# Another order for the first tiles of a four-layer adaptive FFN kernel: router weights loaded first, scores behind tile 0's router, mixing and first diagonal product inside convolutions, weights' transposes at tile 2

## The reference

```
x = x + L0_ffn(L0_cond(x, c))
x = x + L1_ffn(L1_cond(x, c))
x = x + L2_ffn(L2_cond(x, c))
x = x + L3_ffn(L3_cond(x, c))
```

## Time and profile before

| | us |
|---|---|
| median of 3 runs | 742.98 |
| lowest, highest | 742.76, 746.0 |
| the profiled execution, its own time | 743.95 |
| its span, first to last instruction | 742.2 |
| TensorE busy | 727.5 (98% of the span) |
| VectorE, ScalarE, GpSimd busy | 462.0, 300.0, 344.8 |

### The profile page before, as it was taken

How to read it: one execution, slowest core, us unless ns; L and a number is a source line. 1 busy time by engine, 2 the same in 40 slices (tenths; PEclk the granted TensorE clock), 3 DMA queues, 4 the chain that set the end, 5 groups by cost and what they waited for, 6 DMA issues and landing times.

```text
span 742.2 us, 11037 instructions
## 1 busy us (share of the span) xinstructions
PE 727.5 (98%) x3550; PEld 591.3 (80%) x3566; DVE 462.0 (62%) x1060; ACT 300.0 (40%) x577; POOL 344.8 (46%) x386
## 2 busy tenths in 40 slices
PE   9899999999999999999999999999999999999997
PEld 5687777877788888888888888877788887888886
DVE  4976667678622345663477345886678888755533
ACT  5644445444432333254334334232544344534321
POOL 3556677676425512121221015867654645464630
PEclk9999999999999999999999999999999999999999
DMA  8666447544051022110220102424513212221200
GB/s 277 130 139 172 151 135 213 157 143 143 29 184 57 29 62 80 58 29 1 86 99 16 30 37 64 170 58 128 172 44 114 73 44 72 59 87 44 72 29 29
DMA packets 44775, 68.91 MB, mean 93 GB/s; under 512 B 21248, under 2 KB 21600, under 8 KB 44464
## 3 DMA queue, kind: packets, MB, share of 16 engines
q1 hardware_dynamic: 34816, 37.77, 16.9%
q0 software_dynamic: 9152, 29.69, 13.1%
q10 hardware_dynamic: 752, 0.74, 0.3%
HBM read 45.03 MB, written 17.65 MB: 84 GB/s over the span
## 4 chain that ended last, share of the span: by engine, by line
PE 82%; DVE 5%; POOL 5%; DMA 3%; issue 3%; ACT 1%; SPq 0%; DVEq 0%; POOLq 0%; ACTq 0%
PE bank L2232 21%; PE bank L2215 13%; PE bank L2183 12%; PE bank L2088 11%; PE bank L1873 8%; PE bank L1804 4%; PE bank L1909 3%; PE bank L2194 2%; POOL wur L698 2%; PE bank L1943 2%; DMA tap<-in_x_taps_dram 1%; DMA raw<-in_w_dram 1%; PE bank L1921 1%; PE bank L2045 1%; PE bank L2108 1%
## 5 line engine op out<-in xcount | busy, mean ns | idle before, releaser
L1656 DVE TENSOR_TENSOR sil<-bank,sil 128x512 f32<-128x512 f32 x56 | 38.6, 689 | 95.2 <-PE bank L2232 95.2
L2232 PE MATMUL bank<-th,wgr 128*128 128x512 f32 x224 | 88.3, 394 | 1.0 <-DVE tl L1444 1.0
L2232 PE MATMUL bank<-th,wur 128*128 128x512 f32 x224 | 87.7, 391 | 0.0
L2088 PE MATMUL bank<-wda,hh 128*128 128x512 f32 x224 | 87.6, 391 | 0.0
L2232 PE MATMUL bank<-tl,wgr 128*128 128x512 f32 x224 | 87.4, 390 | 0.0
L2232 PE MATMUL bank<-tl,wur 128*128 128x512 f32 x224 | 87.3, 390 | 0.0
L2088 PE MATMUL bank<-wda,hl 128*128 128x512 f32 x224 | 87.3, 390 | 0.0
L2183 PE MATMUL bank<-wda,xch 128*128 (+1 forms) x272 | 84.6, 393 | 0.0
L1111 ACT ACTIVATE hh<-sil 128x512 fp32r<-128x512 f32 x56 | 35.4, 632 | 115.2 <-DVE sil L1656 115.2
L1103 ACT ACTIVATE sil<-bank 128x512 f32<-128x512 f32 x56 | 33.4, 597 | 93.8 <-PE bank L2232 93.7
L1658 DVE TENSOR_TENSOR hl<-sil,hh 128x512 fp32r<-128x512 f32 x56 | 46.3, 826 | 39.1 <-ACT hh L1111 39.1
(11 more groups left out here) (365 smaller groups left out, 1782.4 us busy)
## 6 DMA issues: line engine op xcount, KB each, us to landing
tap<-in_x_taps_dram SPq DMA_DIRECT2D x16, 260.0 KB, 2.9
xin<-in_x_rows_dram SPq DMA_DIRECT2D x16, 256.0 KB, 3.1
xd<-xo SPq DMA_DIRECT2D x16, 256.0 KB, 3.2
xc<-xd SPq DMA_DIRECT2D x16, 256.0 KB, 4.2
xres<-xd SPq DMA_DIRECT2D x4, 1024.0 KB, 5.5
xd<-xres SPq DMA_DIRECT2D x4, 1024.0 KB, 5.0
tsd<-tf SPq DMA_DIRECT2D x4, 1024.0 KB, 4.2
raw<-in_w_dram POOLq DMA_DIRECT2D x16, 256.0 KB, 3.1
```

What stands on the lines that cost most here:

```text
L1656: v.tensor_tensor(hf[:, m % 2], p_pre[(2 * m + 1) % 3][:], sil[:, m % 2], ALU.mult).then_inc(s_hf, 1)
L2088: last = mm(p_acc[j][:], h[:, m % HSLOTS, j * P:(j + 1) * P], wda[:, m * D:(m + 1) * D], start=(m == 0 and n == 0), stop=(m == MT - 1 and ...
L2232: last = mm(p_pre[(2 * m + b) % 3][:], w[:, (m * KT + kt) * P:(m * KT + kt + 1) * P], x[:, kt], start=(kt == 0 and n == 0), stop=(kt == KT ...
```

## The change

The loads are issued in another order and partly from another queue: the router weights and the MLP tensors right behind tap 0 on SyncE, the three condition tensors on ScalarE's queue; the rest of the mixing matrices go ahead of w1_raw. Fewer filler matmuls are issued (12, 2 and 2, where there were 14, 4, 4 and 3). conv(t) does its nine matmuls grouped by part (hi x hi, hi x lo, lo x hi) instead of by shift, for all tiles, and can call another function after the first group: mixed(0) inside conv(2), mix1(0) inside conv(3). lora(t) is grouped by part too and waits for its low part only before the last group. scores go behind router(0), mixing_weights behind router(1), mixed(1) and mixed(2) behind conv(2) and lora(1). hidden(0) goes ahead of positions(1). weights_t and scales_t stand between conv(3) and base(2), the copies to wq are made by ScalarE instead of VectorE, and the scales use bank 4 instead of bank 6. The lists of the other engines follow: w0_hi on ScalarE goes ahead of hid2 and of gate_exp(0), an activation that loads the exponent table stands behind w0_hi(1), weight_scales on VectorE goes to tile 1's step ahead of hidden_lo(1), softmax_two behind t0_lo(1), and GpSimd does x1_lo(0), x1_bias(0) and tap_lo(3) before the weight rounds, and the first table product between the third and fourth round.

```diff
--- before.py
+++ after.py
...
             load_tap(0)
-            sp.dma_start(condt[:], cond_t).then_inc(d_cond, 16)
-            sp.dma_start(cw4[:], cw_t).then_inc(d_cond, 16)
-            sp.dma_start(fs4[:], fside).then_inc(d_cond, 16)
             sp.dma_start(ga_raw[:], l0_ga).then_inc(d_ga, 16)
+            sp.dma_start(mw01[:], mlp_w01).then_inc(d_mlp, 16)
+            sp.dma_start(mw2[:], mlp_w2).then_inc(d_mlp, 16)
+            sp.dma_start(mb01[:], mlp_b01).then_inc(d_mlp, 16)
+            sp.dma_start(mb2[:], mlp_b2.partition_broadcast(BATCH)).then_inc(d_mlp, 16)
+            load_tap(1)
+            sp.dma_start(w0_raw[:], l0_w).then_inc(d_w0, 16)
             sp.dma_start(mixr[:, 0], mix_w[:, 0]).then_inc(d_mix, 16)
-            sp.dma_start(w0_raw[:], l0_w).then_inc(d_w0, 16)
-            load_tap(1)
             sp.dma_start(lb_raw[:], l0_lb).then_inc(d_lb, 16)
+            load_tap(2)
             load_xin(0)
+            sp.wait_ge(d_mix, 16)
+            sp.dma_start(mixr[:, 1:], mix_w[:, 1:]).then_inc(d_mix, 16)
             sp.dma_start(w1_raw[:], l1_w).then_inc(d_w1, 16)
             load_xin(1)
             sp.dma_start(b1b[:], l1_b.partition_broadcast(P)).then_inc(d_b1b, 16)
-            load_tap(2)
-            sp.wait_ge(d_mix, 16)
-            sp.dma_start(mixr[:, 1:], mix_w[:, 1:]).then_inc(d_mix, 16)
...
             rounded(w0h[:, 3], w0_raw[:, 3], s_w0p)
-            pool.wait_ge(s_mix, 2)
+            pool.wait_ge(d_mix, 16)
+            rounded(mixh[:, 0], mixr[:, 0], s_mixh)
             pool.wait_ge(s_hm, 1)
             pool.wait_ge(d_mix, 32)
-            rounded(mixh[:, 1:], mixr[:, 1:], s_mix)
+            rounded(mixh[:, 1:], mixr[:, 1:], s_mixh)
             tap_lo(2)
+            x1_lo(0)
+            x1_bias(0)
+            tap_lo(3)
             pool.wait_ge(s_sw, 1)
-            for k in range(KT):
+
+            def weight_round(k):
                 nc.gpsimd.tensor_scalar(w1_raw[:, k], w1_raw[:, k], wsc[:, 2, k:k + 1], MAGIC, ALU.mult, ALU.add).then_inc(s_wqf, 1)
-            x1_lo(0)
+
+            weight_round(0)
+            weight_round(1)
+            weight_round(2)
             diag_tile(0)
+            weight_round(3)
             diag_lo(0)
-            tap_lo(3)
             diag_tile(1)
-            x1_bias(0)
...
             act.dma_start(conv_raw[:], conv_w).then_inc(d_conv, 16)
-            act.dma_start(mw01[:], mlp_w01).then_inc(d_mlp, 16)
-            act.dma_start(mw2[:], mlp_w2).then_inc(d_mlp, 16)
-            act.dma_start(mb01[:], mlp_b01).then_inc(d_mlp, 16)
-            act.dma_start(mb2[:], mlp_b2.partition_broadcast(BATCH)).then_inc(d_mlp, 16)
+            act.dma_start(condt[:], cond_t).then_inc(d_cond, 16)
+            act.dma_start(cw4[:], cw_t).then_inc(d_cond, 16)
+            act.dma_start(fs4[:], fside).then_inc(d_cond, 16)
...
             t0_hi(0)
+            tap_hi(1)
+            act.wait_ge(d_w0, 16)
+            w0_hi(0)
             act.wait_ge(s_m1, 2 * COND_LAYERS + 1)
             for l in range(COND_LAYERS):
                 nc.scalar.activation(hid2[:, l], bank[6][:, l * BATCH:(l + 1) * BATCH], ACT.Gelu,
                                      bias=mb01[:, l, 1:2]).then_inc(s_g1, 1)
-            tap_hi(1)
-
-            def w0_hi(k):
-                nc.scalar.activation(w0h[:, k], w0_raw[:, k], ACT.Copy).then_inc(s_w0s, 1)
+            w0_hi(1)
+            nc.scalar.activation(rt[:, 192:193], ones[:, 0:1], ACT.Exp)
...
                 x1_hi(t - 1)
                 diag_hi1(t - 1)
+                if t == 2:
+                    for k in range(KT):
+                        act.wait_ge(s_wqt, k // 2 * 2 + 2)
+                        nc.scalar.activation(wq[:, k], bank[6 - k // 2][:].bitcast(BF16)[:, (k % 2) * D:(k % 2 + 1) * D],
+                                             ACT.Copy).then_inc(s_wqc, 1)
                 gate_exp(t)
...
+            gate_exp(0)
             act.wait_ge(s_at, 1)
             nc.scalar.activation(atte[:], att[:], ACT.Exp).then_inc(s_g1, 1)
-            act.wait_ge(d_w0, 16)
-            w0_hi(0)
-            gate_exp(0)
-            w0_hi(1)
+            act.wait_ge(d_lb, 16)
+            nc.scalar.activation(lbh[:], lb_raw[:], ACT.Copy).then_inc(s_lbs, 1)
             conv_out(1)
             act.wait_ge(s_const, 9)
             nc.scalar.activation(identb[:], ident[:], ACT.Copy).then_inc(s_atc, 1)
+            hidden_hi(0)
+            t0_hi(1)
+            tap_hi(2)
             act.wait_ge(s_att, 1)
             nc.scalar.activation(attt[:].rearrange("k l b -> k (l b)"), bank[5][0:3 * CH, 0:COND_LAYERS * BATCH],
                                  ACT.Copy).then_inc(s_atc, 1)
-            act.wait_ge(d_lb, 16)
-            nc.scalar.activation(lbh[:], lb_raw[:], ACT.Copy).then_inc(s_lbs, 1)
-            t0_hi(1)
-            hidden_hi(0)
             mixed(0)
-            tap_hi(2)
+            x1_hi(0)
+            gate_exp(1)
+            conv_out(2)
+            tap_hi(3)
             mixed(1)
-            gate_exp(1)
-            x1_hi(0)
-            conv_out(2)
-            mixed(2)
-            tap_hi(3)
-            diag_hi1(0)
             t0_hi(2)
             hidden_hi(1)
+            mixed(2)
+            diag_hi1(0)
             mixed1(0)
             for t in range(2, TILES):
...
...
                 gating(t, t - 2 if t >= 2 else None)
                 gated(t)
                 if t == 1:
-                    weight_integers()
+                    weight_scales()
                 hidden_lo(t)
                 if t + 1 < TILES:
                     t0_lo(t + 1)
                 if t == 1:
                     for k in range(KT):
-                        dve.wait_ge(s_wqt, k // 2 * 2 + 2)
-                        v.tensor_copy(wq[:, k], bank[6 - k // 2][:].bitcast(BF16)[:, (k % 2) * D:(k % 2 + 1) * D]).then_inc(s_wqc, 1)
+                        dve.wait_ge(s_wqf, k + 1)
+                        v.tensor_scalar(wq_rows[:, k], w1_raw[:, k], MAGIC, QMAX, ALU.subtract, ALU.min).then_inc(s_wqr, 1)
                 if t >= 2:
...
+            w0_lo(0)
+            w0_lo(1)
+            gating(0, None)
+            w0_lo(2)
             softmax_one()
-            softmax_two()
-            gating(0, None)
-            for k in range(KT):
-                w0_lo(k)
+            w0_lo(3)
             gated(0)
             dve.wait_ge(s_lbs, 1)
             v.tensor_tensor(lbl[:], lb_raw[:], lbh[:].bitcast(F32), ALU.subtract).then_inc(s_lbs, 1)
             hidden_lo(0)
             t0_lo(1)
-            mix_rows(slice(1, COND_LAYERS), 3)
-            weight_scales()
+            softmax_two()
+            mix_rows(slice(0, 1), 1)
+            mix_rows(slice(1, COND_LAYERS), 2)
             for t in range(1, TILES):
                 step(t)
...
+            def conv(t, between=None):
+
+                pe.wait_ge(s_taph, t + 1)
+                pe.wait_ge(s_cvw, 1)
                 if t >= 1:
                     pe.wait_ge(s_cvs, t)
-                n = 0
-                for s in range(SHIFTS):
-                    for w, x in parts((cvh[:, s], cvl[:, s]), (taph[:, :, s:s + P], tapl[:, :, s:s + P])):
-                        last = mm(p_cv[:].rearrange("p (b n) -> p b n", b=BPT), w, x, start=(n == 0), stop=(n == 3 * SHIFTS - 1))
-                        n += 1
+                for n, (w, x) in enumerate(((cvh, taph), (cvh, tapl), (cvl, taph))):
+                    if n == 1 and between:
+                        between()
+                    if n == 1:
+                        pe.wait_ge(s_tapl, t + 1)
+                    if n == 2 and t == 0:
+                        pe.wait_ge(s_cvw, 2)
+                    for s in range(SHIFTS):
+                        last = mm(p_cv[:].rearrange("p (b n) -> p b n", b=BPT), w[:, s], x[:, :, s:s + P],
+                                  start=(n == 0 and s == 0), stop=(n == 2 and s == SHIFTS - 1))
                 last.then_inc(s_cv, 1)
...
+            def side_scale():
...
+            keep_busy(12)
             conv(0)
-            pe.wait_ge(d_cond, 48)
-            mm(bank[7][:, 0:BATCH], cw4[:], condt[:], start=True, stop=True).then_inc(s_m1, 1)
+            side_scale()
             pe.wait_ge(d_mlp, 64)
             for l in range(COND_LAYERS):
                 mm(bank[5][:, l * BATCH:(l + 1) * BATCH], mw01[:, l, 0], condt[:], start=True, stop=True).then_inc(s_m1, 1)
-            keep_busy(4)
+            keep_busy(2)
             pe.wait_ge(s_const, 9)
             positions(0)
             pe.wait_ge(s_g1, COND_LAYERS + 1)
             for l in range(COND_LAYERS):
                 mm(bank[6][:, l * BATCH:(l + 1) * BATCH], mw01[:, l, 1], hid1[:, l], start=True, stop=True).then_inc(s_m1, 1)
-            keep_busy(4)
+            keep_busy(2)
...
+                pe.wait_ge(s_hth, t + 1)
+                for n, (x, w) in enumerate(((0, lbh), (0, lbl), (1, lbh))):
+                    if n == 1 and t == 0:
+                        pe.wait_ge(s_lbs, 2)
```

(31 more changed lines are left out.)

35 lines of the change are left out of this document (10 added, 25 removed).

## The result

The changed kernel takes 746.78 us (median; 743.62 to 748.66), the kernel before, run beside it, 743.74 us (742.4 to 748.28): ratio 1.0032, 95% interval 1.0016 to 1.0047. It is slower: by 2.4 us by this ratio, by 3.0 us by the two medians. The prediction was 740.6 us, with a range of 738.9 to 742.7, and a gain where there is a loss.

What follows compares the result with a forecast made beforehand. TensorE was taken to bound the kernel, the question being when base(2) starts: 3.1 us of waits and 1.4 at the start gone, some 2.1 of new waits, so 2.4 off 742.98: 740.6 us, range 738.9 to 742.7.

Steps and rivals of the forecast that it cites:

- The start: Up to tile 0's router: fewer fillers and reordered loads start router(0) at 13.15 instead of 14.53, 1.4 us won.
- the bounds on the MLP weights: MLP weights on SP's queue: last one lands at 9.4 us, bounds 7.5 to 10.5; costs nothing up to 9.9.
- Tile 1: New waits behind VectorE's gating and weight_scales leave TensorE about 1.3 us idle in lora(1), bounds 0.6 to 2.2.
- one gating stall in gating(1): Tile 1, VectorE beside GpSimd: one stall charged, hm(1) at 30.6; bounds no stall to two stalls.
- The rule that I weighed, every such operation hit: Tile 1: VectorE and GpSimd exclude each other in every such gating operation; lora(1) ends 1.3 us later, 1.3 less gain.
- the sum: Clock carried through the new order: base(2) at 40.45 against 42.86, 2.4 us earlier, giving 740.6 us.
- 3.1 us of waits are gone: TensorE's four waits behind tile 0's router, 0.64, 0.93, 1.29 and 0.26, together 3.1 us, counted as removed.
- Rival 3: The clock falls between 9.0 and 13.15 us; 4.3 us of work takes twice as long, 744.9; chance 0.06.
- whether everything behind it moves by the same amount: Behind base(2): nothing is edited and from tile 3 the order is old, so its 2.4 us carries to the median.
- forecast gain 2.4: Whole kernel: base(2) 2.4 us earlier, taken off the median 742.98; gain of 1.5 to 3.7 given 0.57.

Runs made afterwards that it cites:

- experiment 12: Changed kernel with GpSimd held back in tile 1 and stage 2, first table product ahead of the weight roundings, hid2 ahead of w0_hi(0): 741.71 us, ratio 0.9967.
- experiment 6: Kernel before, with GpSimd's late weight split 11 in stage 2 waiting for the class-order table: 743.59 us, ratio 1.0002.
- experiment 1: Changed kernel with GpSimd's x1_lo(0), x1_bias(0) and tap_lo(3) waiting for hm(1): 742.56 us, ratio 0.9989.
- experiment 3: Changed kernel with the weight scales' reduction over the first 128 of 512 columns only: 744.01 us, ratio 0.999.
- experiment 13: Changed kernel with unused identity products filling TensorE's waits, 23 in tile 1 and 30 ahead of the class-order product: 743.85 us, ratio 1.0001.
- experiment 14: Changed kernel with unused identity products filling TensorE's waits in tile 1 alone, 23 of them: 743.36 us, ratio 0.9991.
- experiment 2: Changed kernel with weight_scales moved behind hidden_lo(1) and t0_lo(2) on VectorE: 747.72 us, ratio 1.0057.
- experiment 9: Changed kernel with the path of the layer-1 weights put back to tile 1; loads, scores and the mixing's place as changed: 747.14 us, ratio 1.0055.

## Why the prediction was wrong

**The start: right.** It was early up to tile 0's router and 0.5 us late from base(0) on: conv(0) at 6.24 (I said 6.65 with 0.427 us for a filler; from 1.53 on twelve of them take 0.39 each, and the fourteen of the kernel before took 0.40), the MLP products not waited for, router(0) at 12.61 (13.15), base(0) at 17.89 (17.45), lora(0) at 21.79 (21.25), router(1) at 23.29 (22.75). In the 12 profiled executions that have this start unchanged (experiment 12 alters it), router(1) lies between 21.84 and 23.58, with the first w0h at 12.01 to 14.17; in the three of the kernel before and in experiment 6 it lies between 25.89 and 26.03. My 22.75 is near the middle of the 12. Of the bounds on the MLP weights the low side held: the last of them landed 4.9 us after its issue, at 8.2, not 9.4. The Trainium skill's rule ("DMA: Bandwidth & Descriptors", "Queues, rings and completion order"), that a DMA engine takes turns between queue rows, would have made them about a microsecond late by my estimate; the trace shows no lateness. w0_raw landed at 13.9, not 13.0, and cost 0.94 us at the scores, as the text said it might.

**Tile 1: the step that failed.** I charged one gating stall in gating(1) and put hm(1) at 30.6. It ended at 32.7. There were three: L1375, L1378 and L1380 take 3.3 us together here and 0.8 in experiment 1, so they lose 2.5. My one stall was that of L1365 in the kernel before, 1.33 us for an operation of 0.15, so about 1.2. I had priced the stall rightly and its number wrongly. The text put x1_lo and x1_bias beside the gating and left out tap_lo(3), which stands behind them on GpSimd and caught the third operation. The chain of VectorE's small operations is 3.2 us long undisturbed and 5.7 here, with 3.9 us of GpSimd's work beside it. The rule that I weighed, every such operation hit, gave 1.3 us more than my one stall, and 2.5 less 1.2 is that 1.3; of the rest of the 2.1 us 0.5 is the later router(1). The Trainium skill states the rule in "SBUF — State Buffer", "SBUF: two separate sides", for VectorE operations with two SBUF inputs or in a 2-port mode. The trace agrees for L1380, which has two such inputs. L1375 and L1378 have one tensor and scalars from SBUF and were held as well; whether they ran in such a mode the trace doesn't show.

**From there the sum went on, nearly right, from a wrong number.** The reduction took its 2.27, hts-lo was done 1.9 us later than forecast (35.62, not 33.7), bd1l 2.6 later (39.63, not 37.05; GpSimd's four roundings took 3.4 us and not the 2.7 of the kernel before), base(2) 2.7 later. Counted from router(1), where the execution's start drops out, tile 1 took 19.9 us and not 17.7, and experiments 1 and 3 give back 1.5 and 1.7 of these 2.2. I had taken "3.1 us of waits are gone" for a gain. But hm(1) was in time in the kernel before only because TensorE came late, and the change starts gating(1) 2.0 us earlier (27.00, not 29.05), only for the GpSimd work of tile 1 to be put beside it. In the kernel before, too, TensorE's longest wait in tile 1, 1.29 us, is for VectorE's integers; no experiment there shortened that list. I read TensorE for its waits, and VectorE only for its durations.

**The clock: right mechanism, wrong place and chance.** Rival 3 looked for the fall at 9 to 13 us, gave it 0.06, and cited the full clock of the one profile against it. At 9 to 13 it never fell. It fell behind waits: those of tile 1, and the class order's. From 30 to 36 us TensorE is busy for 3.9 of the 6 us in both profiles of the changed kernel, only one of which falls there; in the kernel before the idle time comes later, with 2.5 of the 4 us from 34 to 38 busy, and two of its three unaltered profiles fall behind it. (The Trainium skill, "TensorE: Matmul & The Clock Gate", "Part 1: The HAM clock gate", says that a monitor of the engine's recent activity sets the clock; that 21 of 22 runs keep the clock with tile 1's waits filled agrees.) One profile of a clean run hid that one run in five of the kernel before is already disturbed; its three times, 742.76, 742.98 and 746.0, had said so.

**The tail: "whether everything behind it moves by the same amount" was assumed.** It does up to 502 us in the two profiles first compared (458.8 and 458.9 us from base(2)); then it depends on whether one transfer is late.

**The account, as an estimate.** Kernel before, with its clock kept, 743.4; forecast gain 2.4: 741.0; tile 1 takes 2.2 us more from router(1) to base(2) than forecast: 743.2. The changed kernel's four runs with the clock kept have a median of 744.0. The 0.8 that is left has the size of the class-order wait (1 to 1.5), but no such run of the unaltered changed kernel was profiled, so this is not shown. The clock's falls, in 15 of 19 runs, bring their median to 747.0, 3.0 us more.

**Open.** Why that weight transfer takes 4.5 to 5.1 us in all three profiles of the kernel before and in experiments 13 and 14, and at most 3.5 in the changed kernel and in experiments 1, 2, 3 and 9. It was the same in every repeated profile of one program (three and two of them), and experiments 13 and 14 have it with the changed order; no run isolates its cause. Open too is how much of the clock's loss each place makes: one execution per program was profiled, and for the others only the mean clock is known.

## What to carry to other kernels

Before you count a wait that a change removes as won, follow the engine that released it: if its list is full, the wait comes back one step later, and moving another engine's two-input work beside its small operations makes that list longer. Look at the spread of the times shown and at the granted clock of several runs, not only at one clean profile: a change that bunches TensorE's idle time can lose more by the clock than by the waits. Where such a gap can't be closed, a few useless products in it hold the clock; where there is no gap they cost time.

## What the runs showed of the hardware

- A VectorE operation of 28 columns beside a GpSimd subtraction or addition of 512 or 520 columns took 0.89 to 1.22 us instead of 0.19 to 0.30, until that operation ended, also where it read one tensor and otherwise only scalars per partition.
- A fall of the granted clock (to 0.50 in windows of 1 us) lasts some 3.4 us here, in one execution 6.8, and costs 0.6 to 1.9 us. It does not come in every execution of the same program.
- 23 products of 128 columns in three waits of 0.5 to 0.8 us held the clock in 21 of 22 runs.
- The same 256 KB transfer at the same place needs up to 3.5 us in one program and 4.5 to 5.1 in another.
- In executions with the same order of loads one 1024 KB load (w0_raw) was there by 12.01 us in one and waited for until 14.17 in another; router(1) came at 21.84 and at 23.58.
